# A decoder block on one core: the cross-attention query split inside its PSUM bank, and rows of minus the maximum turned in one transpose

## The reference

```python
x = _layernorm(x + _L0_attn_ref(x, ...), axis=-1)
# in it: query = heads(ct_q @ Wu_q + b) + heads(_rope(ct_q @ Wq_r + b)); key alike; value = ct_kv @ Wu_v + b
#        attn = softmax(query @ key.T / scale); out = attn @ value; out @ Wo + b
x = _layernorm(x + _L0_xattn_ref(x, ctx_1024, ctx_1024, mask, ...), axis=-1)
# in it: q = (query @ W0.T + b0), k, v from the context; scores where mask == 0 -> -1e9; softmax; @ v; @ W3.T
x = _layernorm(x + _L0_ffn_ref(x, choice_w, w1, w2), axis=-1)
# in it: probs = softmax(x @ choice_w.T); G, I = top_k(probs.T, 256); out.at[I].add(G * (silu(x[I] @ w1) @ w2))
```

## Time and profile before

| | |
|---|---|
| median of 3 runs | 1840.87 us |
| the profiled execution | 1838.62 us, span 1836.5 us |
| PE busy | 1602.8 us (87%) |
| DVE busy | 1241.5 us (68%) |
| ACT busy | 888.1 us (48%) |
| POOL busy | 431.8 us (24%) |
| mean granted TensorE clock | 0.926 of full |

### The profile page before, as it was taken

The page is one execution under the profiler, slowest core; times in us unless marked ns, Lnnn a source line. Parts: engine busy times, 40 slices in busy tenths (PEclk is TensorE's granted clock), DMA queues, the critical chain, the costliest instruction groups (busy, mean ns, idle before and its releaser), DMA issues. The chain is left out here.

```text
span 1836.5 us, 26832 instructions
## 1 busy us (share of the span) xinstructions
PE 1602.8 (87%) x9790; PEld 789.6 (43%) x9790; DVE 1241.5 (68%) x2136; ACT 888.1 (48%) x1582; POOL 431.8 (24%) x543
## 2 busy tenths in 40 slices
PE   7499999797999997979999979899997687999993
PEld 3023324445223244452332444523323436888872
DVE  5588854875788758757888587578877644664443
ACT  2067784351677742526777425267774251111111
POOL 4300003402000035011000350110002301566663
PEclk9589999897999998978999989789999797999996
DMA  5800001814000018231000182310000413455594
GB/s 183 183 8 1 2 1 55 207 45 114 20 1 2 1 50 207 51 93 41 2 1 2 44 208 56 93 41 1 1 2 12 111 48 104 85 106 115 113 266 115
DMA packets 108255, 128.21 MB, mean 70 GB/s; under 512 B 17244, under 2 KB 81756, under 8 KB 108124
## 3 DMA queue, kind: packets, MB, share of 16 engines
q1 hardware_dynamic: 95836, 109.71, 21.7%
q0 software_dynamic: 12288, 16.79, 5.5%
HBM read 84.49 MB, written 40.79 MB: 68 GB/s over the span
## 5 line engine op out<-in xcount | busy, mean ns | idle before, releaser
L965 ACT ACTIVATE pT<-banks 128x512 f32<-128x512 f32 x1184 | 645.1, 595 | 280.1 <-PE banks L1639 167.8
L1172 DVE TENSOR_REDUCE nmf<-banks 128x1 f32<-128x1024 f32 x512 | 604.8, 1220 | 138.9 <-PE banks L1581 137.7
L1639 PE MATMUL banks<-qst,kst 99*128 99x512 bf16 x1024 | 350.3, 389 | 16.5 <-DMA qst<-nmT 7.1
L1581 PE MATMUL banks<-kst,qst 96*128 96x512 bf16 x1024 | 327.9, 405 | 33.0 <-DMA kst<-k_parts 23.0
L1673 PE MATMUL banks<-pT,V 128*32 128x512 f32 x2048 | 274.6, 608 | 17.3 <-ACT oT L953 12.2
L1639 PEld LDWEIGHTS banks<-qst,kst 99*128 99x128 bf16 x1024 | 96.0, 97 | 310.8 <-ACT pT L965 186.7
L784 POOL CAST nmp<-nmf 128x16 bf16<-128x16 f32 x64 | 12.8, 200 | 834.3 <-issue 760.9
L1581 PEld LDWEIGHTS banks<-kst,qst 96*128 96x128 bf16 x1024 | 98.6, 101 | 149.2 <-DVE nmf L1172 37.1
L1167 DVE TENSOR_REDUCE nmf<-banks 128x4 f32<-128x616 f32 x128 | 99.8, 798 | 62.7 <-PE banks L1575 55.1
L1041 ACT ACTIVATE kst<-banks 128x512 f32<-128x512 f32 x64 | 38.1, 597 | 203.3 <-PE banks L1903 177.3
L973 ACT ACTIVATE nmT<-banks 6x1024 bf16<-6x1024 bf16 x64 | 64.8, 1013 | 135.0 <-PE banks L1623 111.0
(11 more groups left out here) (201 smaller groups left out, 2218.0 us busy)
## 6 DMA issues: line engine op xcount, KB each, us to landing
qst<-q_parts SPq DMA_DIRECT2D x48, 256.0 KB, 6.4
kst<-k_parts SPq DMA_DIRECT2D x48, 256.0 KB, 4.5
qst<-in_w SPq DMA_DIRECT2D x16, 512.0 KB
qxs<-in_w SPq DMA_DIRECT2D x16, 512.0 KB
q_parts<-kst SPq DMA_DIRECT2D x48, 128.0 KB, 2.4
qxs<-qx_parts SPq DMA_DIRECT2D x24, 256.0 KB, 4.9
qst<-qx_parts SPq DMA_DIRECT2D x24, 256.0 KB
kst<-in_xT SPq DMA_DIRECT2D x4, 1024.0 KB, 5.0
```

Of the source, the lines that this page charges most:

```text
L965: act.activation(pT[:, n % RING_P, :], PS[:, banks[what, n], :], ACT.Exp, scale=scale).then_inc(s_ex, 1)
L1172: dve.tensor_reduce(nmf[:, m % 2, j, t:t + 1], scores.rearrange("p a n -> p (a n)"), AX.X, ALU.max, negate=True).then_inc(s_smu, 1)
L1581: ins = pe.matmul(pair[:, half, :], qst[0:KQ, h, t * P:(t + 1) * P], kst[0:KQ, h, half * N:(half + 1) * N], start=True, stop=True)
L1639: ins = pe.matmul(ps, kst[0:KM, head, kc * P:(kc + 1) * P], qst[0:KM, head, cols], start=True, stop=True)
```

## The change

- PE makes the first half of the next query before `x1T`; `qx` products 0 and 1 come before the second half, 2 and 3 after the values. Products' banks are renumbered accordingly.
- A `qx` product stays in its bank. ACT rounds it to a bf16 part, with the bias (`cross_part`); PE adds minus that part into the bank (`subtract`, one bf16 matmul with `minusb`, minus the identity); ACT rounds again, and a third time. POOL has no part in it. Products 2 and 3 finish inside the cross stage, behind `smax` 1 and 3.
- Its parts go from SBUF into the stack, 6 DMAs of 128 KB for each of 4 products, without DRAM. SP's order is new, and the q loads of the first 8 heads now stand behind all stores, ahead of group 1's minus-maximum load; the key thirds move one group later.
- A turn is one transpose of 48 columns into 48 rows of 128. ACT's copy is [48 x 128], and the load writes 256-byte runs.
- ACT copies the values from PSUM, POOL adds their bias in place. The addition for the cross residual, that bias, the mask and the self residual move between the groups of `split_max`.
- Logits: the weights are the 8 gate columns, the tokens move through, in four column groups; DVE transposes the result in 32 x 32 blocks first.

```diff
@@ -59,11 +59,14 @@
...
-OPERANDS = [("q", "D")] * 8 + [("k", "D")] * 8 + [("v", "D")] * 4
+HALF_Q = [("q", "D")] * 4
+KEYS = [("k", "D")] * 8
+VALUES = [("v", "A")] * 4
 CONTEXT = [("kx", "A"), ("vx", "D"), ("vxr", "D")]
...
 OUT_SELF = [("oT", "DA"[n % 2]) for n in range(4)] + [("y", "D")] * 4
-INTO_CROSS = [("x1T", "A")] * 4 + [("qx", "A")] * 4
+TURNED = [("x1T", "A")] * 4
+HALF_X = [("qx", "A")] * 2
@@ -85,8 +88,9 @@
...
-EACH = Plan(OUT_SELF + LATENTS + INTO_CROSS + OPERANDS, OUT_CROSS + CONTEXT + ROUTING)
-LAST = Plan(OUT_SELF + INTO_CROSS, OUT_CROSS + ROUTING)
+EACH = Plan(OUT_SELF + LATENTS + HALF_Q + TURNED + HALF_X + HALF_Q + KEYS + VALUES + HALF_X,
+            OUT_CROSS + CONTEXT + ROUTING)
+LAST = Plan(OUT_SELF + TURNED + HALF_X * 2, OUT_CROSS + ROUTING)
@@ -329,9 +336,9 @@
...
-        nmr = sb("nmr", [P, T, G])
-        nmp = sb("nmp", [P, 2, T, 3 * G], BF16)
-        nmT = sb("nmT", [3 * G, 2, S], BF16)
+        nmr = sb("nmr", [P, G * T])
+        nmp = sb("nmp", [P, 2, 3 * G * T], BF16)
+        nmT = sb("nmT", [3 * G * T, 2, P], BF16)
@@ -355,7 +362,9 @@
...
+        xparts_at = early[:, 2 * N:8 * N].bitcast(BF16).rearrange("p (i k n) -> p i k n", i=4, k=3)
@@ -572,18 +586,14 @@
...
-                sp.dma_start(rows[KQ:KM, :, :], nmT[:, n % 2, :]).then_inc(s_nl[n % 2], 16)
+                sp.dma_start(rows[KQ:KM, :, :].rearrange("k h (t n) -> k (h t) n", n=P), nmT[:, n % 2, :]).then_inc(s_nl[n % 2], 16)
@@ -618,37 +628,39 @@
...
+                def load_cross(i):
+
+                    mc, half = divmod(i, 2)
+                    rows = qxs[:, :, :] if mc == 0 else heads_of(qst, 1)
+                    wait_apart(sp, s_eva, at.taken("A", at.nth("qx", i) + 1))
+                    for t, term in enumerate(TERMS):
+                        sp.dma_start(rows[t:KQ:len(TERMS), :, half * N:(half + 1) * N], xparts_at[:, i, term[0], :]
+                                     ).then_inc(s_qx[i], 16)
+
+                wait_apart(sp, s_ql[0], b * 96 + 96, s_ql[1], b * 96 + 96, s_kl[0], b * 96 + 96, s_kl[1], b * 96 + 96)
...
-                    store_cross(range(9, 13))
+                    store_piece((b + 1, 0))
+                    store_piece((b + 1, 1))
                     load_cross(0)
-
-                    wait_apart(sp, s_ql[0], b * 96 + 96, s_ql[1], b * 96 + 96, s_kl[0], b * 96 + 96,
-                               s_kl[1], b * 96 + 96)
-                    store_front(b + 1, range(4))
                     load_cross(1)
-                    stored(b + 1, 3)
-                    load_stack(heads_of(qst, 0), q_parts, 0, 0, s_ql[0])
-                    store_front(b + 1, range(4, 8))
+                    for i in range(2, 6):
+                        store_piece((b + 1, i))
+                    load_cross(2)
+                    load_cross(3)
+                    store_piece((b + 1, 6))
+                    store_piece((b + 1, 7))
...
+                    for i in range(4):
+                        load_cross(i)
...
-                    if more and g < NG - 1:
-                        load_keys(b + 1, range(g - 1, g))
+                    if more and g == 1:
+                        stored((b + 1, 7))
+                        load_stack(heads_of(qst, 0), q_parts, 0, 0, s_ql[0])
+                    elif more:
+                        load_keys(b + 1, range(g - 2, g - 1))
                     load_minus_max(b, NG + g, cross_rows(g))
@@ -826,31 +851,35 @@
...
-                pool.wait_ge(s_ln, b * 2 * T + T)
-                pool.tensor_tensor(xb[:, :, :], z[:, :, :], brow[:, 3:4, :].to_broadcast([P, T, D]),
-                                   ALU.add).then_inc(s_xb, 1)
-                split(b, 9, 13)
-                if more:
-                    split(b + 1, 0, 8)
-                split_max(b, SM_SELF, NG, SM_CROSS // NG, range(1 if not more else NG))
+                split([(b + 1, i) for i in range(8)] if more else [])
+                cross, own = SM_CROSS // NG, SM_SELF // NG
+                split_max(b, SM_SELF, NG, cross, range(1))
...
-                    split_max(b, SM_SELF, NG, SM_CROSS // NG, range(1, NG))
+                split_max(b, SM_SELF, NG, cross, range(1, 2))
+                after_layernorm(b)
+                split_max(b, SM_SELF, NG, cross, range(2, 4))
                 if more:
-                    split_max(b + 1, 0, 0, SM_SELF // NG, range(1))
+                    bias_values(b + 1)
+                split_max(b, SM_SELF, NG, cross, range(4, NG))
+                if more:
+                    split_max(b + 1, 0, 0, own, range(1))
...
-                    split(b + 1, 8, 9)
+                    split([(b + 1, 8)])
+                    split_max(b + 1, 0, 0, own, range(1, 2))
                     mask_bias(b + 1)
+                    split_max(b + 1, 0, 0, own, range(2, 3))
                     residual(b + 1)
-                    split_max(b + 1, 0, 0, SM_SELF // NG, range(1, NG))
+                    split_max(b + 1, 0, 0, own, range(3, NG))
@@ -892,41 +921,61 @@
...
+            def cross_part(at, b, i, part):
...
+                    act.wait_ge(s_xs[i], 2 * b + part)
+                ins = act.activation(xparts_at[:, i, part, :], PS[:, at.bank(idx), :], ACT.Identity,
+                                     bias=bcol[:, 12 + i // 2:13 + i // 2])
+                ins.then_inc(s_xt[i] if part < 2 else s_eva, 1)
...
+            def values(at):
+                for k in range(4):
+                    idx = at.nth("v", k)
+                    taken_before(at, idx)
+                    act.activation(V[:, 2 * k:2 * k + 2, :, 0:HD],
+                                   PS[:, at.bank(idx), :].rearrange("p (t h d) -> p t h d", t=2, d=HD),
+                                   ACT.Copy).then_inc(s_eva, 1)
@@ -1005,22 +1058,47 @@
...
-                parts(at, b, 9, 13)
                 if more:
-                    parts(at, b + 1, 0, 8)
+                    part1(at, (b + 1, 0))
+                    part1(at, (b + 1, 1))
+                    cross_part(at, b, 0, 0)
+                    part2((b + 1, 0))
+                    cross_part(at, b, 1, 0)
+                    part2((b + 1, 1))
+                    for part in (1, 2):
+                        cross_part(at, b, 0, part)
+                        cross_part(at, b, 1, part)
+                    parts(at, [(b + 1, i) for i in range(2, 6)])
+                    values(at)
+                    cross_part(at, b, 2, 0)
+                    part1(at, (b + 1, 6))
+                    part1(at, (b + 1, 7))
+                    cross_part(at, b, 3, 0)
+                    part2((b + 1, 6))
+                    part2((b + 1, 7))
+                    for part in (1, 2):
+                        cross_part(at, b, 2, part)
+                        cross_part(at, b, 3, part)
+                else:
+                    for i, part in ((0, 0), (1, 0), (0, 1), (1, 1), (2, 0), (3, 0), (0, 2), (1, 2),
+                                    (2, 1), (3, 1), (2, 2), (3, 2)):
+                        cross_part(at, b, i, part)
@@ -1240,7 +1307,8 @@
...
-                lgp = PS[:, at.bank(idx), 0:T * E].rearrange("p (t e) -> p t e", e=E)
+                link(dve.transpose(blocks[:, 0:T * V32], PS[:, at.bank(idx), 0:T * V32]))
+                lgp = blocks[:, 0:T * V32].rearrange("p (t e) -> p t e", e=V32)[:, :, 0:E]
                 link(dve.tensor_reduce(lgm[:, :], lgp, AX.X, ALU.max))
@@ -1604,6 +1671,9 @@
                 for what, n in order:
                     if what == "smax":
                         maximum(b, n0, n, cross)
+                        if order is ORDER_AHEAD and n in (1, 3):
+                            for i in (2, 3):
+                                subtract(at, b, i, n // 2)
@@ -1616,11 +1686,12 @@
...
+                        if cross and n == 0:
+                            taken_upto(at, at.nth("qx", 3) + 1)
                         pe.wait_ge(s_nm, b * 2 * NG + m + 1)
                         bank_free(what, n)
-                        rows = PS[0:3 * G, banks[what, n], :].bitcast(BF16)
-                        for t in range(T):
-                            ins = pe.transpose(rows[:, t * P:(t + 1) * P], nmp[:, m % 2, t, :], identb[:, :])
+                        rows = PS[0:3 * G * T, banks[what, n], :].bitcast(BF16)
+                        ins = pe.transpose(rows[:, 0:P], nmp[:, m % 2, :], identb[:, :])
@@ -1764,11 +1837,20 @@
...
+            def subtract(at, b, i, part):
+
+                pe.wait_ge(s_xt[i], 2 * b + part + 1)
+                pe.matmul(PS[:, at.bank(at.nth("qx", i)), :], minusb[:, :], xparts_at[:, i, part, :],
+                          start=False, stop=True, skip_group_check=True).then_inc(s_xs[i], 1)
@@ -1810,10 +1897,12 @@
...
-                for t in range(T):
-                    for c in range(C):
-                        ins = pe.matmul(ps[:, t * E:(t + 1) * E], xT[:, c, t * P:(t + 1) * P], wch[:, c, :],
-                                        start=(c == 0), stop=(c == C - 1))
```

(49 more changed lines are left out.)

252 lines of the change are left out of this document (130 added, 122 removed).

## The result

The changed kernel takes 1823.66 us (median of 4 runs, 1820.11 to 1826.45) where the kernel before takes 1841.46 (4 runs, 1837.96 to 1842.86): 0.9903 of it, 95% interval 0.9883 to 0.9923. That is 17.8 us less. The forecast was 1816, 25 us less, with a range of 1793 to 1832. In a second set of runs the same kernel gave 0.9894 (0.9878 to 0.9911), 1820.88 against 1841.25 us.

What follows compares the result with a forecast made beforehand. PE, busy 87% of the span, was taken as the bound outside the transitions. Terms -17.2 + 1.2 - 4.7 - 2.9 = -23.6 us made 1815.0 from 1838.62, forecast 1816 for a median; range 1793 to 1832.

Steps and rivals of the forecast that it cites:

- turns, eight stages: Single transpose and shorter ACT copy save 17.2 us over four self stages and 1.9 us in a cross stage.
- logits: Logits as 8 matmuls in column groups save 4.7 us in the last batch, 0 in the other three.
- front, transitions and moved GpSimd work: Self to cross: per batch 0.5 us later plus 1.8 us of slow clock; moved POOL work zero, 0.6 last batch.
- DVE's side of the transition: Self to cross: DVE ends `roped` at 1073.0, not 1078.6; PE can start the cross stage 7.7 us earlier.
- SP's queue: Cross stage start: q loads delay group 1's rows, about 7 us of idle PE, front part 0.5 us later.
- Clock: After PE's idle gap in the cross stage, 3.7 us at half speed cost 1.8 us a batch.
- Last batch: Between the last self and cross stages nothing changes; eight cross turns less 0.6 us for `after_layernorm` give -2.9 us.
- the pick: Last batch, between the stages: starts at 1430.0, as before (1430.2), so 0 gained.
- The earlier start carries through: Rival, transitions: SP's chain has slack, each batch gains 5.6 us and keeps its clock; 1794 us, chance 0.19.
- The turns give only their transposes: Rival, turns: something else, ACT's exp or DVE's maxima, closes up; 1826 us, chance 0.15.
- The clogging of SP's queue: Rival, cross stage start: 12 cross loads take 20.3 us to issue, not 7.6; +12.7 us a batch, 1854, chance 0.06.
- The short runs: Rival: 256-byte runs double the 3.78 us load wait at seven places; +26 us, 1842, no change, chance 0.04.

Runs made afterwards that it cites:

- the turns alone: Kernel before with only the single transpose per turn, its split, copy and row load; old front and logits: 1815.54 us, 0.9858.
- the front alone: Changed kernel with single turn and new logits taken back, keeping the new self-to-cross transition and moved GpSimd work: 1854.00 us, 1.0071 of the kernel before.
- The run with that load ahead: Changed kernel with query loads behind group 3's rows, plus next self stage's group 0 rows ahead of x: 1777.32 us, 0.9645; again 1775.63.
- another order of the queue: Changed kernel with query loads behind group 1's rows (1799.27 us, 0.9774) or behind group 3's rows (1797.46 us, 0.9767), key loads later.

## Why the prediction was right, and where its size was off

The direction, the case and most places held. By its steps, with the single parts' times (a forecast for the front is the sum without turns: 3 x (0.5 + 1.8) + 0.6; turns: 17.2 + 3 x 1.9 + 3.5):

| step | forecast | measured |
|---|---|---|
| turns, eight stages | -26.4 | -25.7 |
| logits | -4.7 | -5.7 |
| front, transitions and moved GpSimd work | +7.5 | +13.6 |
| sum | -23.6 | -17.8 |

The whole change gave -17.8 us in one set of runs and -20.4 in the other.

**Turns: right in seven stages, wrong in the last cross stage.** 0.56 us a turn in the steady self stage (0.63 was taken), 0.4 in the cross stage (0.48), a copy of 269 ns (280). By stages the turns alone gave 17.0 us in the self stages (17.2 forecast), 6.0 in cross stages 0 to 2 (5.7) and nothing in cross stage 3, where the forecast had 3.5. That the medians' 25.7 still comes so near to 26.4 is in part luck: the profiled executions, whose stages these are, differ by 21.8. The bursts came 3.01 us apart, just above the 2.84 to 2.95 named.

**DVE's side of the transition: right.** `roped` ends 49.1, 48.9 and 50.5 us behind the turned heads in batches 0 to 2 (48.7 forecast), PE starts at 49.4, 50.0 and 50.8 (49.3).

**SP's queue: right in its order, mis-sized in one term.** The last store was forecast to be issued 67.3 us behind the turned heads; it was issued at 67.8, 67.0 and 69.6, and SP went on to the query loads 1.9 to 3.2 us later, as the forecast's 1.9 to 4.4 allows. The step that failed is "6 q loads, 1.5 MB, which at some 235 GB/s take 6.5 us, with some 1.2 us before them": 7.7 us from their issue to group 1's rows. It is 9.7, 10.2 and 9.9 us. So the copy of turn 3 comes 1.3, 3.3 and 3.6 us later than before, 2.7 on the mean where the forecast had 0.5: 6.6 us over three batches. The front alone is 6.1 us off its forecast, but by its stages only some 4.5 of that lie in the three transitions (11.4 us against 6.9), where its turn-3 copy comes 1.5, 3.1 and 2.0 us later than before; another 2.8 lie in the last cross stage (3.4 against 0.6), and differences of 3 us each way in the self stages belong to no step of it. The windows read 180 GB/s while these loads were issued and 221 behind, where the forecast had 235; by these rates the 1.5 MB take some 1 us more, an estimate. What else stood ahead of the rows in the DMA engines was not separated.

**Clock: near, a little too low.** From the restart to turn 4, batch 2, the changed kernel lost another 2.3 us at the 0.50 level; forecast 1.8. A stretch that the forecast did not name, from 1073.20 to 1080.10 us, had a granted clock of 0.51 too (from 1081 to 1085 us before it was 0.50), behind PE's wait of 1.82 us for the second part of product 2. PE stands still behind it for the rows all the same.

**Logits: right.** 4.6 us nearer in the last batch, nothing in the other three, where the load behind the context keys sets the start. The run with that load ahead shows that the order alone held 6.5 to 7.8 us a stage.

**Last batch: wrong.** 2.9 us less was forecast for its cross stage; it became 0.8 to 2.7 us longer. Turns alone leave it at 127.0 us, as before, and the front alone makes it 130.4. Two steps failed. The forecast counted eight turns, 3.5 us. With the turns alone the stage is 1.6 us shorter from its first product on: 1.5 up to the first value burst (29.5 us, before 31.1) and 0.1 behind it, where three distances between bursts shrink by 0.3 to 0.4 us, the fifth grows from 6.25 to 7.17 and the rest stay. At turn 1 PE waits for POOL, which issues six indirect loads (`tok_g`) ahead of the split, for 4.09 us before and 4.66 now, so what turn 0 saves is lost there. And ahead of its first product the stage is 1.7 us longer, with nothing changed in it; in the first 5 us behind the turned heads the granted clock was 0.68, before 1.00. Timeline of PE, turns 1 and 2 of the last batch in the changed kernel:

```profile
1442.15 0.30 PE L1694 MATMUL banks<-identb,nmp 128*48 128x128 bf16 x1 [4.70 <-POOL nmp L802]
1447.68 0.30 PE L1694 MATMUL banks<-identb,nmp 128*48 128x128 bf16 x1 [0.89 <-POOL nmp L802]
```

The other step is the pick, forecast 36.2 us behind the turned heads and before at 36.4. It comes at 39.0 and 39.3, because `rank_chosen` comes at 32.6 and 33.0 us, not 29.8, since the subtractions wait for ACT one by one. The first cross product comes 1.4 and 1.8 us later than before; but with the turns alone it is 1.7 us later too, so this is not shown to be the front's. The moved `after_layernorm` adds 0.89 and 1.45 us of waiting at turn 2 (0.6 was taken). How much of the rest is clock stays open.

**The rivals.** "The earlier start carries through" was refuted by the 6.8 us gap, and is near with another order of the queue (1794 against 1797.5 and 1799.3). "The turns give only their transposes" was refuted by the turns alone. The clogging of SP's queue did not occur: 12 cross loads took 7.64 to 9.04 us to issue in batches 0 and 1, where that rival had 20.3. The short runs cost nothing that shows: 12 KB took 2.8 to 3.7 us from issue to use with them and 3.8 to 3.9 with long runs. The Trainium skill (DMA: Bandwidth & Descriptors, Specifications) says that below 512 bytes the engine falls short of its rate. No run here shows a cost of that.

## What to carry to other kernels

When work is moved so that an engine is ready earlier, list what each queue issues between the old and the new ready time, small loads with a waiter first: three loads of 12 KB behind 1.5 MB each cost 21.6 to 23.4 us here, and moving the bulk behind them turned a change of 1% into one of 2.3%. A second reordering of the same queue, of a wait that the old kernel could have lost as well, made it 3.6%. A bulk load goes behind the last small load that someone waits for soon, not where its own data become ready. Time the parts of a change one by one: a part that loses hides well behind one that gains.

## What the runs showed of the hardware

A 12 KB load on SP's queue took 2.8 to 3.9 us from its issue to its reader with two loads of 256 KB directly ahead of it, and 5.7 to 6.3 with six. The granted clock of TensorE in a stage whose code was not touched differed between kernels: 0.87 and 0.91 from the first product of cross stage 3 on, which with its transition took 131.0 and 127.8 us, and 0.50 and 0.68 in the first 5 us of it. Differences under 3 us in one stage of one profile say little.
